# Building the last five destination tiles of two edge tables with GpSimd's indirect adding transfers, beside the dense build and the dense experts

## The reference

```
# layer 2: softmax-weighted sum over edges; layer 3: weighted sum over edges
score = s_src[src] + s_dst[dst]; e = exp(-lrelu(score))
num   = segment_sum(e[:, None] * h[dst], src, num_segments=n)     # L2
agg   = segment_sum(hw[src] * sym_norm[:, None], dst, ...)        # L3
```

## Time and profile before

| | us |
|---|---|
| median of 3 runs | 4425.66 (4422.83 to 4426.33) |
| the profiled execution | 4438.98 |
| its span | 4437.5 |
| PE busy | 3031.0 (68%) |
| DVE busy | 2545.3 (57%) |
| ACT busy | 1118.0 (25%) |
| POOL busy | 1418.9 (32%) |

### The profile page before, as it was taken

How to read it: one execution, slowest core, us unless ns; L and a number is a source line. 1 busy time by engine, 2 the same in 40 slices (tenths; PEclk the granted TensorE clock), 3 DMA queues, 4 the chain that set the end, 5 groups by cost and what they waited for, 6 DMA issues and landing times. The chain is left out here.

```text
span 4437.5 us, 49631 instructions
## 1 busy us (share of the span) xinstructions
PE 3031.0 (68%) x14277; PEld 2242.9 (51%) x14277; DVE 2545.3 (57%) x4638; ACT 1118.0 (25%) x2246; POOL 1418.9 (32%) x1393
## 2 busy tenths in 40 slices
PE   4234554545454543884888858999967996699598
PEld 2111211112121222663888856777746885588487
DVE  7457777877777745344999963111134666233333
ACT  1111111111111102220455533333324552000122
POOL 4666666666666624343600000000000000001233
PEclk8667667766777675996999977999988998799799
DMA  2466666666666644343444442000037443655333
GB/s 93 151 188 191 194 193 196 195 198 192 195 197 193 191 129 162 66 68 90 175 177 177 177 174 75 12 12 12 6 101 141 143 134 107 243 176 184 101 66 53
DMA packets 289833, 613.00 MB, mean 138 GB/s; under 512 B 52204, under 2 KB 195696, under 8 KB 279760
## 3 DMA queue, kind: packets, MB, share of 16 engines
q0 software_dynamic: 105584, 294.01, 24.5%
q1 hardware_dynamic: 166800, 267.12, 17.5%
q10 hardware_dynamic: 17360, 50.80, 3.8%
HBM read 437.46 MB, written 176.95 MB: 138 GB/s over the span
## 5 line engine op out<-in xcount | busy, mean ns | idle before, releaser
L2056 PE MATMUL gnn_p_msg<-gnn_msg,gnn_ident 128*128 128x512 f32 x928 | 673.6, 893 | 764.6 <-DVE gnn_msg L2144 414.8
L2009 POOL DMA_INDIRECT gnn_got<-kv,gnn_index x928 | 880.0, 948 | 455.4 <-issue 304.5
L2056 PEld LDWEIGHTS gnn_p_msg<-gnn_msg,gnn_ident 128*128 128x128 f32 x928 | 258.9, 293 | 1178.7 <-issue 1149.8
L2525 PE MATMUL tables_p_pair<-tables_spread,tables_hot 128*128 128x100 f32 x3328 | 398.9, 279 | 20.2 <-DVE tables_spread L2499 16.8
L2525 PEld LDWEIGHTS tables_p_pair<-tables_spread,tables_hot 128*128 128x128 f32 x3328 | 384.6, 194 | 34.2 <-DVE tables_spread L2499 30.2
L2130 DVE TENSOR_TENSOR gnn_prod<-gnn_got,gnn_p_both 128x2048 f32<-128x2048 f32 x116 | 265.4, 2288 | 225.4 <-issue 173.8
L746 DVE SCALAR_TENSOR_TENSOR ffn_acc<-ffn_pC,ffn_gates,ffn_acc 128x256 f32<-128x256 f32 x200 | 88.9, 480 | 395.7 <-PE ffn_pC L597 395.7
L2806 PE MATMUL gnn_p_sum<-gnn_hs,gnn_edge 128*128 x2500 | 288.9, 278 | 32.2 <-DVE gnn_edge L2836 32.0
L2144 DVE TENSOR_TENSOR gnn_msg<-gnn_got,gnn_p_both 128x2048 f32<-128x2048 f32 x116 | 264.7, 2282 | 74.3 <-ACT gnn_p_both L2037 43.5
L2806 PEld LDWEIGHTS gnn_p_sum<-gnn_hs,gnn_edge 128*128 128x128 f32 x2500 | 285.4, 194 | 37.0 <-issue 36.2
L1150 PE MATMUL ffn_pA<-ffn_hw,ffn_slabs 128*128 128x256 f32 x1250 | 274.3, 381 | 33.8 <-DMA ffn_beta<-in_L_ffn_beta 33.8
(11 more groups left out here) (417 smaller groups left out, 4551.3 us busy)
## 6 DMA issues: line engine op xcount, KB each, us to landing
weight_table<-tables_weight_slab SPq DMA_DIRECT2D x13, 3200.0 KB
count_table<-tables_count_row SPq DMA_DIRECT2D x13, 3200.0 KB
ffn_slabs<-weight_table SPq DMA_DIRECT2D x25, 1600.0 KB, 7.1
gnn_cell<-count_table ACTq DMA_DIRECT2D x50, 576.0 KB, 3.8
state<-gnn_out SPq DMA_DIRECT2D x116, 136.0 KB
ffn_xs<-by_expert SPq DMA_DIRECT2D x60, 260.0 KB, 3.3
gnn_got<-kv,gnn_index POOLq DMA_INDIRECT x928
ffn_x<-x SPq DMA_DIRECT2D x20, 640.0 KB, 5.6
```

What stands on the lines that cost most here:

```text
L2009: pool.indirect_dma_start(out=got[k][:, r, :], out_offset=None, in_=kv_dram, in_offset=rows_at(index[k][:, r:r + 1])).then_inc(gathered[k] ...
L2056: last = nc.tensor.matmul(p_msg[k][:], ident[:], msg[k][:, r:r + 2].rearrange("p r h d -> p (r h d)"), start=(r == 0), stop=(r == R - 2))
L2525: last = nc.tensor.matmul(at, hot[c % AHEAD][:, r, :], spread[c % AHEAD][:, r, :], start=True, stop=True)
```

## The change

Only 20 of the 25 destination tiles are still built densely (`PAIRS` is 10). The cells of the last five (`LATE`) are cleared by SP during `ffn0` (16.4 MB of zeros from a 128 x 640 buffer that GpSimd sets), their addresses and values are computed by VectorE at the end of `find_slots`, and GpSimd adds them: for each of the 64 slots, each of the two tables and each of the five tiles, one indirect adding transfer of 128 single cells, 640 in all. Before the next slot of the same table it waits until the previous slot's five have landed. The first 18 slots (180 transfers) stand in `tables` behind the 50 neighbour gathers, the other 46 (460 transfers) in `ffn1` behind the preamble. Slots that a node doesn't have add 0 to a spare column of its own. The diff, cut:

```diff
 # sparse_moe_phase, SyncE, behind the base stores and ahead of the wait for the plan
+                if clear:
+                    sp.wait_ge(pool_set, 1)
+                    for late_rows in clear[1]:
+                        sp.dma_start(late_rows.rearrange("(p n m) a -> p n (m a)", p=P, m=clear[0].shape[1]),
+                                     clear[0][:].rearrange("p (a m) -> p a m", a=1)
+                                     .to_broadcast([P, LATE * NP // clear[0].shape[1], clear[0].shape[1]]))\
+                            .then_inc(cells_cleared, 16)
 ...
+                if clear:
+                    sp.wait_ge(cells_cleared, 16 * len(clear[1]))
 # sparse_moe_phase, GpSimd
+                if clear:
+                    pool.memset(clear[0][:], 0.0)
 ...
 TABLE_TILES = TILES + 1
+DENSE = 20
+LATE = TILES - DENSE
+BESIDE_TABLES = 18
 ...
 # find_slots
-        pool.iota(slot[:], [[1, SLOTS]], base=0, channel_multiplier=0, allow_small_or_imprecise_dtypes=True)\
-            .then_inc(slot_set, 1)
+        pool.iota(spare[:], [[-1, SLOTS]], base=NP - 1, channel_multiplier=0, allow_small_or_imprecise_dtypes=True)
+        pool.iota(node_i[:], [[P, LATE]], base=DENSE * P, channel_multiplier=1)
+        pool.iota(tile_i[:], [[1, LATE]], base=DENSE, channel_multiplier=0)
+        pool.iota(slot[:], [[1, SLOTS]], base=0, channel_multiplier=0, allow_small_or_imprecise_dtypes=True)
+        pool.drain().then_inc(slot_set, 1)
 ...
             dve.drain()
+            find_cells(dve)
+
+    def find_cells(dve):
+        dve.tensor_copy(source[:], link[:, late, :, 0])
+        dve.tensor_scalar(row_base[:], node_i[:], float(NP), None, ALU.mult)
+        dve.scalar_tensor_tensor(slab_base[:], tile_i[:], float(P * NP - P), node_i[:], ALU.mult, ALU.add)
+        dve.drain()
+        dve.tensor_tensor(source[:], source[:], spares, ALU.subtract)
+        dve.drain()
+        dve.tensor_tensor(source[:], source[:], valid[:, late, :], ALU.mult)
+        dve.drain()
+        dve.tensor_tensor(source[:], source[:], spares, ALU.add)
+        dve.drain()
+        dve.tensor_copy(source_i[:], source[:])
+        dve.tensor_tensor(cell_at[:, 0], source[:], by_tile(row_base), ALU.add)
+        dve.drain()
+        dve.tensor_scalar(part[:, late, :], source_i[:], 7, None, ALU.logical_shift_right)
+        dve.drain()
+        dve.tensor_copy(column[:], part[:, late, :])
+        dve.drain()
+        dve.scalar_tensor_tensor(source[:], column[:], float(-P), source[:], ALU.mult, ALU.add)
+        dve.scalar_tensor_tensor(column[:], column[:], float(P), by_tile(slab_base), ALU.mult, ALU.add)
+        dve.drain()
+        dve.scalar_tensor_tensor(cell_at[:, 1], source[:], float(NP), column[:], ALU.mult, ALU.add)
+        dve.tensor_copy(cell_of[:, 0], valid[:, late, :])
+        dve.tensor_tensor(cell_of[:, 1], weight[:, late, :], valid[:, late, :], ALU.mult)
+        dve.drain()
 ...
+def add_cells(s, tables, cell_at, cell_of, s0, s1):
+    added = [s.sem(f"cells_added{j}") for j in range(2)]
+    pool_waited = s.sem("cells_waited")
+    def run(pool):
+        for i in range(s0, s1):
+            for j in range(2):
+                if i > s0:
+                    pool.wait_ge(added[j], (i - s0) * (16 * LATE))
+                    pool.sem_inc(pool_waited, 1)
+                for t in range(LATE):
+                    pool.indirect_dma_start(out=tables[j], in_=cell_of[:, j, t, i:i + 1], in_offset=None,
+                                            out_offset=rows_at(cell_at[:, j, t, i:i + 1]), compute_op=ALU.add)\
+                        .then_inc(added[j], 16)
+        for j in range(2):
+            pool.wait_ge(added[j], (s1 - s0) * (16 * LATE))
+            pool.sem_inc(pool_waited, 1)
+    return run
 # table_phase
-    PAIRS = TABLE_TILES // 2
+    PAIRS = DENSE // 2
 ...
                                                 in_offset=rows_at(at[:, k:k + 1])).then_inc(neighbours_loaded, 16)
+                add_more(pool)          # slots 0 to 17; in moe_phase likewise behind the preamble: slots 18 to 63
                 pool.wait_ge(neighbours_loaded, 32 * TILES)
```

More of the change, by code:

```diff
@@ L292, in moe_phase @@
 def moe_phase(nc, name, ident_dram, left, right, x_dram, mixed_dram, out_dram, router, gate, w1, hidden_act, w2, w3, b3,
-              inner_norm=None):
+              beside, inner_norm=None):
     Ex, _, H = w1.shape
@@ L400, in moe_phase @@
         HID = Ex * 2 * (MB + 2 * deep)
+        add_more = beside(s)
         banks = [(0, 2), (2, 4), (4, 5)]
@@ L763, in sparse_moe_phase @@
 def sparse_moe_phase(nc, name, ident_dram, before_dram, x_dram, out_dram, sorted_dram, router, gate, w1, act_1, b1,
-                     w2, b2, w3, b3, inner_norm=None, slab=None):
+                     w2, b2, w3, b3, inner_norm=None, slab=None, clear=None):
     Ex, _, H = w1.shape
@@ L886, in sparse_moe_phase @@
         base_stored = s.sem("base_stored")
+        cells_cleared = s.sem("cells_cleared")
         all_added = s.sem("all_added")
@@ L1448, in _, with ffn0 @@
                 share_out(block_total(dve))
-def ffn0(nc, a, x, out, by_expert):
+def ffn0(nc, a, x, out, by_expert, clear):
     p = "L0_ffn_"
@@ L1455, in ffn0, with ffn1 @@
                      "softmax_top2_softmax", a[p + "expert_w1"], ACT.Relu, a[p + "expert_b1"],
-                     a[p + "expert_w2"], a[p + "expert_b2"], a[p + "expert_w3"], a[p + "expert_b3"])
-def ffn1(nc, a, left, right, x, mixed, out):
+                     a[p + "expert_w2"], a[p + "expert_b2"], a[p + "expert_w3"], a[p + "expert_b3"], clear=clear)
+def ffn1(nc, a, left, right, x, mixed, out, beside):
     p = "L1_ffn_"
@@ L1462, in ffn1 @@
               [(ACT.Relu, *(a[p + n + str(i)] for n in ("b", "g", "be", "m", "v"))) for i in (1, 2)],
-              a[p + "W2"], a[p + "Wo"], a[p + "bo"])
+              a[p + "W2"], a[p + "Wo"], a[p + "bo"], beside)
 def ffn3(nc, a, x, slab, out, by_expert):
@@ L2323, with find_slots @@
 TABLE_TILES = TILES + 1
+DENSE = 20
+LATE = TILES - DENSE
+BESIDE_TABLES = 18
 SLOT_TILES = TABLE_TILES + 2
 NOWHERE = 999.0
-def find_slots(nc, s, natural, links_dram, slots):
+def find_slots(nc, s, natural, links_dram, slots, cell_at, cell_of):
     low, high, weight = slots[:, 0], slots[:, 1], slots[:, 2]
@@ L2335, in find_slots @@
     valid = s.sb("valid", [P, TILES, SLOTS])
+    late = slice(DENSE, TILES)
+    spare = s.sb("spare", [P, SLOTS])
+    node_i = s.sb("node_i", [P, LATE], i32)
+    tile_i = s.sb("tile_i", [P, LATE], i32)
+    row_base = s.sb("row_base", [P, LATE])
+    slab_base = s.sb("slab_base", [P, LATE])
+    source = s.sb("source", [P, LATE, SLOTS])
+    source_i = s.sb("source_i", [P, LATE, SLOTS], i32)
+    column = s.sb("column", [P, LATE, SLOTS])
     slot_set = s.sem("slot_set")
@@ L2369, in compute, with by_tile @@
             dve.drain()
-    return gather, compute
-def table_phase(nc, name, a, slots, count_rows, weight_slabs, xt_dram, left, right_rows):
+            find_cells(dve)
+    def find_cells(dve):
+        wide = [P, LATE, SLOTS]
+        spares = spare[:].rearrange("p (a s) -> p a s", a=1).to_broadcast(wide)
+        def by_tile(v):
+            return v[:].rearrange("p (t a) -> p t a", a=1).to_broadcast(wide)
+        dve.tensor_copy(source[:], link[:, late, :, 0])
[22 more added lines that the diff above has]
+        dve.drain()
@@ L2376, in table_phase @@
+def table_phase(nc, name, a, slots, count_rows, weight_slabs, xt_dram, left, right_rows, beside):
     CHUNK = 8
     CHUNKS = P // CHUNK
-    PAIRS = TABLE_TILES // 2
+    PAIRS = DENSE // 2
     BOTH = 2 * TILES
@@ L2462, in _ @@
                                                 in_offset=rows_at(at[:, k:k + 1])).then_inc(neighbours_loaded, 16)
+                add_more(pool)
                 pool.wait_ge(neighbours_loaded, 32 * TILES)
@@ L2904, in build_program @@
                          normalize=lambda s, loaded: own_rows(nc, s, loaded, state, place, natural))
[L2905 to L2914, removed]
+        tables = (count_table, weight_table)
@@ new lines, in build_program @@
+        late_rows = [t[DENSE * P * NP:TILES * P * NP, :] for t in tables]
+        with nc.sbuf_tensor("cell_at", [P, 2, LATE, SLOTS], i32) as cell_at, \
+                nc.sbuf_tensor("cell_of", [P, 2, LATE, SLOTS], fp32) as cell_of:
+            with nc.sbuf_tensor("zeros", [P, 640], fp32) as zeros:
+                ffn0(nc, a, xs[1], xs[2], by_expert, (zeros, late_rows))
+            with nc.sbuf_tensor("left", [P, TILES, F + 8], fp32) as left, \
+                    nc.sbuf_tensor("right", [P, TILES, F + 8], fp32) as right:
+                with nc.sbuf_tensor("slots", [P, 3, SLOT_TILES, SLOTS], fp32) as slots:
+                    projection_phase(nc, "xt", ident, xs[2], [a["L1_gnn_weight"]], [xt],
+                                     dots=((a["L1_gnn_attn_l"], 4), (a["L1_gnn_attn_r"], 4)),
+                                     beside=lambda s: find_slots(nc, s, natural, a["links"], slots, cell_at, cell_of))
```

(5 more changed lines are left out.)

## The result

The change made the kernel slower: 4667.05 us (median of 4 runs, 4663.79 to 4679.83) against 4424.24 (median of 4, 4421.7 to 4426.33), ratio 1.0556 [1.054, 1.0572]. The forecast was 4331, rival 1 (the addition is the dear part) 4607. The profiled execution took 4665.67 us, a span of 4664.0.

The account below looks back on a forecast made before the run. Each phase has its own bound: DVE in `tables`, with PE close behind. Profiled: 4438.98 + 6 (addresses) - 101 (`tables`) = 4344, `ffn1` hidden; median: 4425.66 - 95 = 4331 us. Range for 8 in 10: 4312 to 4615.

Parts of the forecast that it names:

- rival 1: Addition is dear: 1.56 us a transfer, 1.86 with the gap; `tables` gains 60, `ffn1` loses 235; 4607 us, chance 0.30.
- the price of an adding transfer: GpSimd in `tables` and `ffn1`: 0.98 us a transfer, 1.28 from one to the next when undisturbed.
- 15 us of slack: In `ffn1`, 460 transfers end after 619 us of the phase's 634.05, so they are hidden.
- The landing: GpSimd's waits inside rounds cost nothing: at least 6.4 us of other transfers cover a landing of 2.2 us.
- ends of phase: After POOL's last transfer in `tables` and `ffn1`: about 2.2 us of landing and 2 us for the barrier.
- Beside DVE: In `tables`, DVE's two-input operations add 0.63 us to each transfer: 1.91 us each; DVE is not slowed.
- rival 3: Beside DVE in `tables`, strictly one transfer a chunk, 2.27 us each: `tables` gains 71, 4361 us, chance 0.09.
- the miss in `tables`: Forecast for `tables`: 153 transfers out beside DVE, 27 alone at 1.28 us, end at 2525, gain 101 us.
- 38.97 us a pair: Dense part of `tables`: a pair of tiles takes 38.97 us, so dropping three takes 116.9 us off the path.
- `xt` 6.5 us longer, 6 forecast: Address arithmetic on DVE's queue in `xt` is on the path and adds 6 us.
- the clearing: 16.4 MB of zeros on SP's queue take 39 us and are hidden; at half the rate they cost 10 us.
- The signs named to tell the cases apart: In `ffn1`: POOL transfers of about 980 ns, or 1560 for rival 1; POOL's last ahead of the last rows' store.

Follow-up runs that it names:

- first three-tile kernel: Changed kernel with only the last three tiles by 384 adding transfers, 132 beside `tables` and 252 beside `ffn1`, one semaphore a table: 4196.21 us, 0.9935 of the kernel before.
- finer wait: One semaphore for each table and tile, not one a table: 4160.15 us (0.9866 of the kernel before) with overwriting transfers, 4434.13 us (1.0521) with the changed kernel's adding ones.
- overwriting kernel: Changed kernel with its 640 transfers overwriting the cell instead of adding to it (no `compute_op`): 4196.4 us, 0.9951 of the kernel before.

## Why the prediction was wrong

**The step that failed: the price of an adding transfer.** The trace bracketed it between 0.98 and 1.56 us and the prediction took "0.98, the row without a check". The addition is 583 ns of it and the check 13, measured each by itself. With 1.55 us rival 1's working holds for `ffn1`, where it gave 869 - 634 = 235 us (measured 244.6), but not for `tables`, where it gave a gain of 60 (measured 13.2). That the addition's further descriptors would be nearly free did not come true. Looking back, the trace of the kernel before leaned the other way: its 60 adding transfers had 144 packets each, its scatters about 47 (44 of them in the window 1685 to 1767, row below), and the check turned out to add none.

```profile
q0 software_dynamic: 2064, 5.73, 19.4%
```

Both rows were one feature away, as the text says; what it left unsaid is how unlike the two bets were. A miss at the low end cost nothing, since `ffn1` had 15 us of slack; a miss at the high end cost 46 us for each 0.1 us. The range reached 4615 and was 52 us too short.

**The landing, the second failure.** "The waits inside the rounds cost nothing ... against a landing of 2.2." In `ffn1` a landing of cells takes 5 to 8 us by the medians above, with the addition or without, and beside the table stores it reached 20.4 us in the first three-tile kernel. The finer wait brought 44 us in the overwriting kernel's two phases (`ffn1` 671.3 - 635.6, `tables` 472.5 - 464.0), 36 of its time, and 23 of the adding one's. The 2.2 us came from one wait of DVE in `ffn0`, and stood for five queued transfers of cells. Even with the price right the kernel stands at 0.9951 of the one before and not at the forecast's 0.979; the finer wait closes about half of that gap. The two ends of phase, 10 to 12 us from POOL's last instruction instead of 4, are the same term.

**Beside DVE.** 1.91 us a transfer was forecast. The overwriting ones came at 2.04 (140 in 285 us), the adding ones at 2.33 in the changed kernel (123 in 286). On the chips of the experiments the median instruction took about 1.96 us with the addition and without it, 1.97 for 64 adding cells, but 897 ns, undisturbed, for 64 overwriting ones. So most transfers either pass at their own price or are held for about a chunk of DVE, and the share that is held differs from kernel to kernel; a fixed 0.63 us on top of any price was the wrong form. What decides it isn't settled by these runs. For the adding transfers rival 3's 2.27 us each was nearer than the forecast's 1.91.

In the changed kernel this gives the miss in `tables`: 123 transfers and not 153 are out by 2484, when DVE is through, and the other 57, not 27, cost 1.86 us each and not 1.28. With the end of 12.5 us instead of 4 the stage goes on for 123 us and not 39, which is 84 of the 88 us that it is off. The gathers, 104 us and not 94, are part of why fewer went out in time.

The Trainium skill ("SBUF — State Buffer", Who interferes with whom) has the port held by DVE for an instruction's whole length; the 1.96 us against 0.97 alone agree, the 897 ns of the 64-cell overwriting transfers beside the same instructions don't by themselves. DVE was hardly slowed in return: it is busy for 264.7 us in 286 with the transfers and for 268.5 in 285 without them, and on the chips of the experiments the last matmul of the dense part starts 392 to 395 us after `tables` began with 640 adding transfers, 391 without any.

**What held.** 38.97 us a pair: 114 us gained without transfers, with 117 less 6 for `find_cells` forecast. `xt` 6.5 us longer, 6 forecast. `ffn0` 351.7 us after 358.5, the clearing hidden. (The working counts seven two-input operations and ten drains for `find_cells` where the diff has eight and nine, which makes no difference, and 39 us of clearing from 1685.5 end at 1725, not 1740.) PE's work untouched (448 of 455 us busy in `ffn1`). The signs named to tell the cases apart, 980 or 1560 ns in `ffn1` and POOL ahead of or behind the end of the other engines' work, told them apart.

## What to carry to other kernels

When everything hangs on one price that the trace brackets, work out at which price the change turns, and what a miss costs on either side, before choosing; here a slack of 15 us stood against a loss of 235. Price a chain of small transfers by three numbers, not one: what writing one costs its engine, what it costs the DMA engines, and how long it takes to land beside the work of that phase. To move work to an idle engine, fill the cover that is there and leave the rest: with the finer wait, 384 of these transfers gain 1.0 to 1.3%, and 640 lose 5.2%.

## What the runs showed of the hardware

- An indirect transfer with addition costs GpSimd 1552 ns for 128 cells, without it 969, with a bounds check 982; at 64 cells 1412 with the addition and 897 without.
- The addition costs the DMA engines more than GpSimd. In the stretches of `ffn1` where little else moves, the engines were busy for 0.51 of 455 us with the adding transfers (244) and for 0.10 of 410 with the overwriting ones (282; stretch below). The queue's own packets, in the same two stretches (last two rows, adding first; packets, MB, share of 16 engines), took 47.3% and 1.6%: about 0.9 us of each engine for an adding transfer against 0.02. The rest of the 0.10 is the phase's own loads and stores, whose packets took 8.7% there and 3.6% beside the adding ones. The 4 bytes of a cell cost about as much as the 1 KB row that was estimated at 1.04, and half the cells about half of it: 29.0% of 400 us for 231 transfers, 0.5 us.

```profile
2600.00:3010.00 410.00, 377.16 (x1496) 286.75 (x1494) 70.16 (x155) 137.76 (x224) 272.37 (x282) 0.95 0.10 10
...
q0 software_dynamic: 35100, 0.14, 47.3%
...
q0 software_dynamic: 8969, 0.16, 1.6%
```

- The queue's packets tell the same: 197744 with the addition, 126064 without it, 105584 without the transfers, so 144 packets for an adding transfer of 128 cells and 32 for an overwriting one. With 64 cells it is 156784 and 126064: 80 packets and again 32.
- From issue to landing, cells of the weight table took longer than those of the count table in `ffn1`: 7.6 against 6.0 us overwriting, 7.5 against 5.0 adding. Why is not shown.
